# Where the second attention layer's keys are computed: in the opening, or in the router stage of the first expert layer

## What is computed

```python
x = x + xattn0(_layernorm(x), ctx, mask)           # 16 heads of 16
x = x + ffn0(_layernorm(x))                        # top-2 router, capacity 32 per expert
x = x + xattn1(_layernorm(x), ctx, attn_mask, pad) # K1 = ctx @ Wk1.T + bk1
x = x + ffn1(_layernorm(x))                        # top-2 of 8 experts
# ffn0: logits = einsum('GSM,ME->GSE', x, router_w)
#       dispatch, combine = _gating_top2(logits, C)
#       expert_inputs = einsum('GSEC,GSM->EGCM', dispatch, x)
```

## Time and profile before

| | us |
|---|---|
| runs | 1242.88 median (1240.97 to 1243.66), 3 runs |
| profiled execution: its own time | 1245.71 |
| profiled execution: span from first to last instruction | 1244.0 |
| TensorE busy in the span | 1145.3 (92%) |
| VectorE, ScalarE, GpSimd busy | 545.8, 450.4, 244.3 |
| opening: its 14 rounds on TensorE | 39.84 to 77.23 |
| attend 0: first matmul, SyncE's mask writes, end of the last matmul | 88.51, 306.53, 325.5 |
| router stage: from SyncE's first issue to SyncE's first issue of the next stage | 342.61 to 382.80 |
| expert stage: TensorE's expert matmuls | 383.23 to 613.2 |

### The profile page before, as it was taken

How to read it: one execution, slowest core, us unless ns; L and a number is a source line. 1 busy time by engine, 2 the same in 40 slices (tenths; PEclk the granted TensorE clock), 3 DMA queues, 4 the chain that set the end, 5 groups by cost and what they waited for, 6 DMA issues and landing times. The chain is left out here.

```text
span 1244.0 us, 19158 instructions
## 1 busy us (share of the span) xinstructions
PE 1145.3 (92%) x7207; PEld 730.1 (59%) x7231; DVE 545.8 (44%) x1553; ACT 450.4 (36%) x591; POOL 244.3 (20%) x366
## 2 busy tenths in 40 slices
PE   7989999999859999999859999999997699999996
PEld 4443333333447888888636333333325599999995
DVE  4757777773362111111156776666505322112121
ACT  4556666666422111111032455555562101110110
POOL 4662222225000000000003100000100233333331
PEclk8999999999959999999989999999999799999998
DMA  7646222001172333345257322220003799999972
GB/s 216 170 150 154 41 43 41 7 1 51 52 272 51 136 135 135 135 159 188 58 188 174 63 40 39 39 40 1 1 2 97 252 372 377 317 322 312 314 227 47
DMA packets 87926, 168.53 MB, mean 135 GB/s; under 512 B 9474, under 2 KB 61396, under 8 KB 85252
## 3 DMA queue, kind: packets, MB, share of 16 engines
q1 hardware_dynamic: 80132, 157.99, 40.2%
q0 software_dynamic: 5152, 6.05, 2.5%
q10 hardware_dynamic: 2560, 3.41, 0.9%
HBM read 147.30 MB, written 20.98 MB: 135 GB/s over the span
## 5 line engine op out<-in xcount | busy, mean ns | idle before, releaser
L1212 ACT ACTIVATE prob<-st_ps 128x1024 f32<-128x1024 f32 x256 | 253.9, 1022 | 188.1 <-PE st_ps L1099 105.2
L219 DVE CUSTOM_DVE_ANT_0 junk<-s_ps,bias_rows,mx 128x512 f32<-128x512 f32 x236 | 168.0, 748 | 64.6 <-PE s_ps L204 63.9
L1091 PE MATMUL st_ps<-q_stack,k_stack 100*128 100x512 bf16 x512 | 184.3, 383 | 7.6 <-ACTq L1189 3.5
L219 DVE CUSTOM_DVE_ANT_0 junk<-s_ps,bias_rows 128x512 f32<-128x512 f32 x232 | 153.3, 689 | 72.6 <-PE s_ps L204 72.1
L204 PE MATMUL s_ps<-k_stack,q_stack 97*128 97x512 bf16 x468 | 175.3, 384 | 6.2 <-ACT q_stack L248 5.4
L1599 PE MATMUL h_ps<-expert_in,w 128*128 (+1 forms) x704 | 155.0, 382 | 2.2 <-PEq L66 2.2
L1599 PEld LDWEIGHTS h_ps<-expert_in,w 128*128 128x128 f32 (+1 forms) x704 | 132.7, 189 | 23.0 <-issue 2.4
L1111 PE MATMUL o_ps<-prob,v_unit 128*32 128x512 f32 x1024 | 139.7, 599 | 1.0 <-ACT prob L1212 1.0
L204 PEld LDWEIGHTS s_ps<-k_stack,q_stack 97*128 97x128 bf16 x468 | 45.0, 98 | 139.1 <-DVE mx L219 83.9
L1945 ACT ACTIVATE silu<-gu_ps 128x512 f32<-128x512 f32 x46 | 27.5, 597 | 226.7 <-PE gu_ps L1886 217.3
L1629 ACT ACTIVATE gelu_out<-h_ps 128x256 f32<-128x256 f32 (+1 forms) x88 | 33.7, 383 | 182.2 <-PE h_ps L1599 182.2
(11 more groups left out here) (283 smaller groups left out, 1182.8 us busy)
## 6 DMA issues: line engine op xcount, KB each, us to landing
wg<-in_gateT SPq DMA_DIRECT2D x23, 1024.0 KB
wu<-in_upT SPq DMA_DIRECT2D x23, 1024.0 KB
wd<-in_downT SPq DMA_DIRECT2D x23, 1024.0 KB
w<-in_w SPq DMA_DIRECT2D x16, 1368.0 KB
w<-in_w SPq DMA_DIRECT2D x8, 1280.0 KB
k_scr<-k_parts SPq DMA_DIRECT2D x48, 128.0 KB, 2.3
k_stack<-k_scr SPq DMA_DIRECT2D x16, 384.0 KB, 5.1
k_stack<-k_scr SPq DMA_DIRECT2D x16, 256.0 KB, 5.7
```

Of the source, the lines that this page charges most:

```text
L219: self.pr.nc.vector.tensor_tensor_reduce(out=self.junk[:, self.bank("job", u, j)], in0=self.ps[:, self.bank("job", u, j)], in1=self.m.bias ...
L1091: pe.matmul(st_ps[:, h], stack(K[b], ROWS, i % 2, h, slice(kt * P, (kt + 1) * P)), stack(Q[b], ROWS, i % 2, h, slice(0, SQ)), start=True, ...
L1212: nc.scalar.activation(prob[:, kt % 2, 2 * hp:2 * hp + 2], st_ps[:, 2 * hp:2 * hp + 2], ACT.Exp).then_inc(exp_done, 1)
```

## The change

The eight key cells of layer 1 leave the opening. It keeps six rounds, each with five or six row jobs and one of the later value tiles, then four jobs of unit 1 (`EARLY` = 4 takes the place of `AHEAD` = 12 there; `row_plan` keeps `AHEAD` as its aim, so attend does the other eight). ScalarE copies the later values out of PSUM without bias, and GpSimd adds the bias in attend. Near the end of attend 0, SyncE loads the context again into the K stack of batch 0 (its last unit is done) and layer 1's key weights into a V tile; GpSimd reorders them. In the router stage the eight cells run on TensorE around the router's matmuls, and are split by ScalarE and GpSimd (the first three remainders by VectorE), into the memory of the stacks; SyncE writes 24 DMAs of parts behind the experts' weights. At the start of the expert stage GpSimd sets the stacks' constant rows again.

```diff
-        cells = [("k", 0, 0, 0), ("k", 0, 0, 1), ("q", 0, 0, 0), ("k", 0, 0, 2), ("k", 0, 0, 3), ("q", 0, 0, 1)]
...
-        JOBS = [(0, j) for j in range(32)] + [(1, j) for j in range(AHEAD)]
-        PER = 3
+        JOBS = [(0, j) for j in range(32)]
+        NEXT = [(1, j) for j in range(EARLY)]
...
-            return JOBS[PER * r:PER * (r + 1)] if r < NC - NA - 1 else JOBS[PER * r:]
+            return JOBS[5 * r + min(r, 2):5 * (r + 1) + min(r + 1, 2)]
...
-                for dt in range(DT):
-                    for b in range(B):
-                        for i in (2 * dt, 2 * dt + 1):
-                            k_out_of(1, i, b, 12 + 4 * dt + 2 * b + 1)
...
-                pool.wait_ge(wk_in[1], 48)
-                g.tensor_copy(by_inner(wk[:, 1]), by_head(wk_raw[1])).then_inc(wk_done[1], 1)
...
-                    if n - NA in (7, 12):
-                        top.cut(pool, row, (n - NA) // 12)
+                    if n == NA + 3:
+                        top.cut(pool, row, 0)
                 low(NC - 1)
+                top.cut(pool, row, 1)
...
                 def value(n):
                     if n < 2:
                         pe.wait_ge(s_yT, 3 + n)
+                    elif n < NV // 2 + 2:
+                        pe.wait_ge(v_done, n - 1)
                     else:
-                        pe.wait_ge(v_done, n - 1)
...
+                pe.wait_ge(const_in, 16 * 2 * B)
+                pe.wait_ge(pr.load[0][0], 16 * N_DMA)
                 for r in range(NC - NA):
                     jobs = jobs_of(r)
+                    row.scores(pe, jobs[:2])
                     cell(NA + r, (0,))
-                    if r == 0:
-                        pe.wait_ge(const_in, 16 * 2 * B)
-                        pe.wait_ge(pr.load[0][0], 16 * N_DMA)
-                    if (1, 0) in jobs:
-                        pe.wait_ge(pr.load[0][1], 16 * N_DMA)
-                    row.scores(pe, jobs[:1])
+                    row.scores(pe, jobs[2:4])
                     cell(NA + r, (1,))
-                    row.scores(pe, jobs[1:])
-                    if r == 9:
+                    row.scores(pe, jobs[4:])
+                    value(NV // 2 + r)
+                    if r == 3:
                         top.turn(pe, 0)
-                for n in range(NV // 2, NV):
-                    value(n)
-                    if n == NV // 2 + 2:
-                        top.turn(pe, 1)
+                pe.wait_ge(pr.load[0][1], 16 * N_DMA)
+                row.scores(pe, NEXT[:2])
+                value(NV - 2)
+                value(NV - 1)
+                row.scores(pe, NEXT[2:])
+                top.turn(pe, 1)
...
+                def value_kept(n):
+                    act.wait_ge(v_ready, n + 1)
+                    a.activation(m.vals[:, n], v_ps[:, n % 2, 0:D], ACT.Copy).then_inc(v_kept, 1)
...
+                    value_kept(NV // 2 + n - NA)
...
-                for n in range(NV // 2, NV):
-                    value_out(n)
+                row.maxima(dve, NEXT)
...
-        plan = row_plan(AHEAD if l == 0 else 0)
+        plan = row_plan(EARLY if l == 0 else 0)
...
+                    sp.wait_ge(st_ready, (NU - 1) * 16)
+                    sp.dma_start(pr.late_ctx(), t["ctxT"].rearrange("(t p) n -> p t n", p=P)).then_inc(pr.late_in, 16)
+                    sp.wait_ge(pv_done, 2 + (NU - 1) * KT)
+                    sp.dma_start(pr.late_wk()[0], t["wkT1"].rearrange("(t p) n -> p t n", p=P)).then_inc(pr.late_in, 16)
+                    bias_in(sp, pr.late_bk, t["bk1"], pr.late_in)
...
+                    nc.gpsimd.tensor_tensor(m.vals[:, KT:], m.vals[:, KT:], m.bv[:].unsqueeze(1).broadcast_to([P, KT, D]),
+                                            ALU.add).then_inc(v_sum, 1)
+                    pool.wait_ge(v_sum, 1)
...
+                    raw, wk = pr.late_wk()
+                    pool.wait_ge(pr.late_in, 64)
+                    nc.gpsimd.tensor_copy(by_inner(wk), by_head(raw)).then_inc(x_bias, 1)
+                    pool.wait_ge(x_bias, 2)
...
+                    for dt in range(DT):
+                        for b in range(B):
+                            last = 4 * dt + 2 * b + 1
+                            sp.wait_ge(hi_done, last + 1)
+                            sp.wait_ge(mid_done, last + 1)
+                            sp.wait_ge(lo_done, last + 1)
+                            for i in (2 * dt, 2 * dt + 1):
+                                keys_out(pr, sp, 1, parts, pr.late_out, i, b)
...
+                    def low(n):
+                        if n < NA:
+                            pool.wait_ge(rest_done, n + 1)
+                        pool.wait_ge(mid_done, n + 1)
+                        g.tensor_tensor(key_part(n, 2), rest_k[:, n % 2], key_part(n, 1), ALU.subtract).then_inc(lo_done, 1)
+                    for n in range(NA):
+                        low(n)
+                    for n in range(NA, NK):
+                        pool.wait_ge(full_done, n - NA + 1)
+                        pool.wait_ge(hi_done, n + 1)
+                        pool.wait_ge(lo_done, n - 1)
+                        g.tensor_tensor(rest_k[:, n % 2], whole[:, n % 2], key_part(n, 0),
+                                        ALU.subtract).then_inc(drest_done, 1)
+                        if n > NA:
+                            low(n - 1)
+                    low(NK - 1)
...
+                    def key_cell(n):
+                        dt, ch = divmod(n, 4)
+                        if n == 0:
+                            pe.wait_ge(pr.late_in, 64)
+                        if n >= 3:
+                            pe.wait_ge(hi_done, n - 2)
+                            if n < NA + 3:
+                                pe.wait_ge(rest_done, n - 2)
+                            else:
+                                pe.wait_ge(full_done, n - 2 - NA)
+                        for k in range(DT):
+                            mm = pe.matmul(kps[:, n % 3], wk[:, k, dt * P:(dt + 1) * P],
+                                           ctx[:, k, ch * 512:(ch + 1) * 512], start=(k == 0), stop=(k == DT - 1))
+                        mm.then_inc(k_ready, 1)
...
+                    key_cell(0)
+                    key_cell(1)
+                    key_cell(2)
                     norm.tensor(pe, tps, logits)
+                    key_cell(3)
+                    key_cell(4)
                     pe.wait_ge(m1_done, 1)
                     pe.matmul(rps[:, 1, 0:NT * E0], pr.lower[:], first[:].rearrange("p g e -> p (g e)"),
                               start=True, stop=True).then_inc(p1_ready, 1)
+                    key_cell(5)
                     pe.wait_ge(m1k_done, 1)
                     pe.matmul(rps[:, 2, 0:NT * E0], pr.lower[:], second[:].rearrange("p g e -> p (g e)"),
                               start=True, stop=False)
                     pe.matmul(rps[:, 2, 0:NT * E0], pr.ones[:], first[:].rearrange("p g e -> p (g e)"),
                               start=False, stop=True).then_inc(p2_ready, 1)
+                    key_cell(6)
+                    key_cell(7)
                     for g in range(NT):
                         pe.wait_ge(disp_done, g + 1)
                         if g >= 2:
                             pe.wait_ge(d_done, g - 1)
+                        else:
+                            pe.wait_ge(hi_done, NK - 2 + g)
+                            pe.wait_ge(full_done, NK - 2 + g - NA)
                         for k in range(DT):
...
+                    def middles(j):
+                        if j >= 1:
+                            middle(j - 1)
+                    norm.scalar(act, tps, highs, middles)
                     act.wait_ge(x_sub, 1)
                     nc.scalar.activation(raw[:], raw[:], ACT.Exp).then_inc(x_exp, 1)
+                    for n in range(NA, NK):
+                        high(n)
+                        full(n)
+                        if n > NA:
+                            middle(n - 1)
+                    middle(NK - 1)
...
+                    for n in range(NA):
+                        dve.wait_ge(hi_done, n + 1)
+                        if n >= 2:
+                            dve.wait_ge(lo_done, n - 1)
+                        v.scalar_tensor_tensor(out=rest_k[:, n % 2], in0=kps[:, n % 3], scalar=key_bias(n),
...
+                nc.gpsimd.memset(pr.V[0][:], 1.0).then_inc(ones_done, 1)
+                pool.wait_ge(pr.late_out, 16 * 3 * NG * B)
+                for b in range(B):
+                    pool.wait_ge(ones_done, 2 * b + 1)
+                    nc.gpsimd.memset(pr.K[b][STACK:ROWS], 1.0).then_inc(ones_done, 1)
+                    pool.wait_ge(ones_done, 2 * b + 2)
+                    nc.gpsimd.memset(pr.Q[b][PADROW:PADROW + 1], 1.0).then_inc(ones_done, 1)
```

More of the change, by code:

```diff
@@ L41 @@
 AHEAD = 12
+EARLY = 4
 TURN_AT = (3, 6)
@@ L754, in tensor, with scalar @@
             use(NT // 2 - 1)
-    def scalar(self, act, ps, between=None):
```

(11 more changed lines are left out.)

134 lines of the change are left out of this document (84 added, 50 removed).

## The result

The changed kernel took 1248.3 us (median of 7 runs, 1246.9 to 1253.29) where the kernel before took 1242.21 (7 runs, 1240.79 to 1245.13). The ratio is 1.0049, 95% interval 1.0034 to 1.0064: slower by 4 to 8 us, against a forecast of +6.2. The two profiled executions differ by less, 1247.9 - 1244.0 = 3.9 us of span.

The account below looks back on a forecast made before the run. TensorE was taken to fill nearly the whole span except stage seams and the router stage, set by a chain. Opening -2.6, attend +1.8 and router +7.0 gave +6.2, shifted to the runs' median 1249.1 us, range 1238 to 1254.

Parts of the forecast that it names:

- The opening: Opening: a gain of 2.6 us, bounds 0.9 and 7, set by when SyncE has issued its last write.
- The stall: Opening: TensorE waits 3.9 us for GpSimd's cut, which stands behind cell 9's remainder; the clock may fall.
- Attend 0: Attend 0: eight more jobs of 0.22 us on TensorE, which is never idle there, +1.8 us.
- Bias addition, late loads and the second turn: Attend 0: GpSimd's addition and SyncE's loads are covered; unit 1's turn costs nothing, 0.5 at its other end.
- The router stage: Router stage: earlier chain start -2.5, GpSimd's operations in the way +10.3, gather -0.8, together +7.0 us.
- The chain: Router stage: VectorE's small operations up to the first gather matrix start 2.5 us earlier, bounds +4 and -4.
- the other bound: Router stage: the clock falls all the same and cells are doubled, bound +4 for the start of VectorE's chain.
- The ports: Router stage: nine of GpSimd's thirteen 1.15 us operations hold VectorE's chain through shared SBUF ports, +10.3 us, bounds 0 and 15.
- The gather: Router stage: it runs at half clock again, 10.2 us, less 0.8 for the chance of partly full clock.
- faster* rival: Router stage: ports do not matter for short operations; router -3.5, whole kernel 1238.6 us; chance 0.22.
- half* rival: Router stage: four or five GpSimd operations in the chain's way, 5 us; router +1.7, whole about 1243.8; chance 0.13.
- cold* rival: Router stage: clock falls before the cells and stays, each cell 3.4 us; whole kernel 1256 us; chance 0.05.

Follow-up runs that it names:

- e6: The changed kernel with twelve instead of four row jobs of the second unit in the opening (`EARLY = 12`); ratio to the kernel before 1.0037.
- e9: e8 with the router stage's first three cells put behind the logits instead of ahead of the turned tokens; ratio to the kernel before 0.9970.
- e5: The kernel before, plus six 512-column matmuls with unread results at the router stage's start; ratio to the kernel before 0.9996.
- e8: e7 plus six query writes issued by ScalarE's queue and eight instead of four jobs in the opening; ratio to the kernel before 0.9908.
- e3: The changed kernel with GpSimd's 13 router-stage subtractions replaced by constant fills, two each; one run, 1242.8 us.
- e4: The changed kernel with the splitting of layer 1's keys and its scratch writes moved to GpSimd in the expert stage; ratio to the kernel before 0.9984.
- e7: The changed kernel with both the edits of e1 and e4; ratio to the kernel before 0.9952.
- e1: The changed kernel with GpSimd's first cut of the row maxima put ahead of cell 9's remainder; ratio to the kernel before 1.0009.
- e2: The changed kernel with each low part of the router stage computed twice by GpSimd, once into an unread buffer; one run, 1261.57 us.

## Why the prediction came out

**The opening.** The stall was forecast at 3.9 us between 58 and 62, with a clock that may fall behind it; it was 4.09, to 61.70, and it fell. SyncE's last issue came at 83.35 instead of 81.8. Attend's first matmul moved by -2.0 in the pair of profiles. Five profiles with this opening give 86.4 to 88.6, mean 87.4; two with the opening of before give 88.5 and 88.9. The gain is thus nearer to -1.3 than to the -2.6 of the sum, within its bounds (-0.9 to -7). The start of the opening's rounds moves by as much from one execution to the next: SyncE's first key write of them came at 56.16 here and at 54.65 in e6.

**Attend 0.** +1.8 forecast, +1.1 measured. The eight matmuls cost their 1.8 (e6), and 0.7 came back. About 0.5 of that is attend's start, where the granted clock stayed at 0.50 for 4.4 us instead of 5.5 (to 90.9 in the one, 94.0 in the other); this is an estimate, and the rest stays open. Bias addition, late loads and the second turn cost nothing, as said.

**The router stage.** +7.0 forecast, +5.0 measured, by terms:
- The chain starts 2.4 us earlier (forecast 2.5), at the full clock that was expected. The prediction's own figures, cells to 348.3 and then 6.4 us, give 354.7, which is 1.7 earlier and not 2.5; the rows would have borne the smaller number, and the hit is partly luck. The reason holds only half: e9 shows that the pause brings the clock down, and e5 that filling it need not save it. The prediction named a clock that falls all the same as the other bound; it came, for a part of the matmuls up to the logits, in six of the ten profiles of other kernels with work in the pause. In the changed kernel it came behind the logits (cells 3 and 4), where it cost the chain nothing; only e8's first profile was free of it.
- The ports: 7.8 us instead of 10.3. This is the term of the sum that was most mis-sized. The mechanism was right and the count as well (nine forecast, ten stretched). The size was not: the prediction charged each turn a whole 1.15 us, but an operation comes while GpSimd's is already under way and waits for the rest of it, 0.78 us on the mean. And reductions, and operations with an input from PSUM, let GpSimd pass, so that in the first stretch of the chain only one in three or four is held.
- The gather: 0.4 us less from the first matrix to the experts' first matmul (14.7 for 15.1), 0.8 forecast. SyncE's last key write was issued by 377.0, under the gather, as said.

**The expert stage** and all behind it moved by 0.3 us, as costed.

**The sum.** By parts -2.0 + 1.1 + 5.0 - 0.3 = +3.9 in the pair of profiles, and with the opening's mean +4.6; the ratio of the runs gives +4 to +8. The median's +6.1 agrees with the forecast of +6.2 better than the parts do, and that closeness is partly luck: router and attend were over-priced by 2.7, the opening's gain was over-priced by 1.3, and the rest lies in the scatter of the runs. The *faster* rival (ports do not matter for short operations) is e3's world: there the stage takes 37.8, 3 us under before. The *half* rival (four or five in the way, router +1.7) falls by its count. The *cold* rival falls by the first cells: 5.39 us for three, not 3.4 each.

## What to carry to other kernels

Before giving an idle engine work beside a chain of another, look whether the two share a port: here 13 subtractions of GpSimd, idle until then, cost a chain of VectorE's small operations 7.8 us, while about the same time in fills cost nearly nothing. Put such work where the other engine has slack (here the expert stage: 7 us back in the chain, 8 in the ratio of the runs). And ask of every instruction that another engine waits for what stands ahead of it on its own: five small operations behind two large ones cost 5 us.

## What the runs showed of the hardware

- A VectorE operation with two SBUF inputs that meets a GpSimd subtraction already under way ends shortly behind it, 0.08 us for 128x64 and 0.28 for 128x256: it takes 0.81 instead of 0.22 us, and 1.28 instead of 0.42. Beside a fill `spot` kept its 0.42. A reduction beside a subtraction keeps its 0.22 us, and so did operations with an input from PSUM (0.22 at 362.32 and 363.44 in the changed kernel). Where both engines have such operations back to back, they alternate, at 1.37 us for VectorE's 0.42 and 1.33 for GpSimd's 1.15.
- TensorE's clock fell from 2.4 to 1.2 GHz in the middle of its own work, not only in a pause: within the first six matmuls after 1.94 us of idle time (7.08 for 5.39 us) in e4, e5 and e7, within the last logits in e4, e5, e6, e7 and e8's second profile (2.8 to 3.4 us for 1.97), and within cells 3 and 4 in the changed kernel, e1, e2 and e3 (5.38 for 3.65), where TensorE had by then worked for 12 us with no pause above 0.5. One kernel gave 36.8 and 39.1 us for the same stage by this alone.
- A pause of 2.6 us ahead of e8's attend and one of 7.9 ahead of the changed kernel's both left the first matmuls there at half clock (0.63 us where 0.38 is usual).
